# Small-head attention: lays ahead of waits, turned peaks in a scores bank, output projection ahead of the next scores

## The chip, the cores and the metric

The kernel runs on one core of one Trainium2 chip. The metric is the device time of one execution in microseconds, lower is better. The times of before are 7645.25, 7623.12 and 7643.76, median 7643.76.

## What is computed

A residual stack of eight blocks on x (32 samples of 128 tokens, 128 features), with a condition vector and a context of 77 tokens for each sample. The change touches attention with 16 heads of 8 features. It occurs once in the experts block (self attention, no mask) and twice in each of the six layers of the fourth conditioning block:

```python
for i in range(6):
    xn = _adaln(x, noise_emb, n1_w[i], n1_b[i])
    q, k, v = ...            # q and k turned by _rope
    a = _attn(q, k, v, src_mask).reshape(B, L, D) @ so_w[i].T
    x = x + a
    xn = _adaln(x, noise_emb, n2_w[i], n2_b[i])
    q = _rope((xn @ cq_w[i].T).reshape(B, L, H, HD))
    k = _rope((context @ ck_w[i].T).reshape(B, LC, H, HD))
    v = (context @ cv_w[i].T).reshape(B, LC, H, HD)
    a = _attn(q, k, v, ctx_mask).reshape(B, L, D) @ co_w[i].T
    x = x + a
    xn = _adaln(x, noise_emb, n3_w[i], n3_b[i])
    x = x + gelu(xn @ f1_w[i].T + f1_b[i]) @ f2_w[i].T + f2_b[i]
```

`_attn` is softmax(q k' / sqrt(8) + mask) v for every sample and head. All is float32.

## The kernel before, in words

Stages follow each other with a barrier between; each writes the queue of every engine by hand, and the engines meet only at semaphores. `stage_attn_experts` (E) holds the small attention of the experts block, `stage_layers` (H) the six layers in a hardware loop: self attention, cross attention, feed-forward.

One **unit** of the small attention is one sample, 32 units (B) in an attention. The 16 heads are four row groups of the TensorE array (32 rows, one PSUM bank each) by four masked key copies `km`. Per unit:

- `scores(u)` on PE: with a mask, four one-row matmuls that lay the mask into banks 0 to 3 (L178), then four matmuls that add the scores (L182).
- `peaks(u)` on DVE (L260): the row maxima, banks 0 and 1 first (this signals `half_peaked`), then 2 and 3. `split_peaks` (L267, L268) makes two bf16 parts of them and signals `peaks_ready`.
- `turn_peaks(u)` on PE (L190) transposes the peaks into columns 0 to 127 of bank PEAKS, which is 7. `spread_peaks(u)` on DVE (L273) makes `shift` from it and signals `shift_ready`.
- `again(u)` on PE computes the scores once more, transposed, keys on partitions, into banks 0, 1, 4 and 5: first four lays of the shift (L202), then 16 matmuls (L206).
- `exponential(u, half)` on ACT (L302), two halves, banks 0 and 1, then 4 and 5, each signals `exp_done`.
- `values(u, half)` on PE (L220) into bank FLAT, which is 6; `flatten` on ACT (L310) copies it out; `flip(u)` on PE (L228) transposes it back; `norm(u)` on DVE (L279, L280) divides by the sums.

Banks 0 and 1 are shared by the scores and by `again`; banks 2 and 3 belong to the scores alone, 4 and 5 to `again` alone.

The order of iteration u on PE is `turn_peaks(u)`, `scores(u+1)`, `values(u-1)` twice, the caller's `meanwhile(u)`, `again(u)`, `flip(u-1)`. On DVE it is `peaks(u)`, `split_peaks(u)`, `meanwhile(u)`, `norm(u-2)`, `spread_peaks(u)`. On ACT: `flatten(u-1)`, `meanwhile(u, 0)`, both exponentials, `meanwhile(u, 1)`.

In the layers `meanwhile` carries the output projection of pairs of units. On PE, `outputs(a, p, 0)` at even u from 4 transposes two samples into columns 256 to 511 of bank 7 (L2592), after waiting for `o_normed` and for `mix_added` of pair p-1; `outputs(a, p, 1)` at odd u from 5 multiplies them by the output weights in the same columns (L2598), after waiting for `oT_ready`. ACT copies between the two (`take_out`, L2729). On DVE, `add_outputs(a, (u-6)//2)` at even u from 6 adds the product to `y_all` (L2824), signals `mix_added` and takes row statistics (L2448); at every fourth u it takes their moments (L2454, L2456). As turned peaks and projection share bank 7, `area_free` makes `turn_peaks` wait until the other engine has left it. In stage E, `meanwhile` is on DVE only: the residual addition of four samples (L1763).

At the start of each attention twelve matmuls of no use (`keep_clock`, L161) follow `scores(0)`.

## Time and profile before

| | |
|---|---|
| times, us | 7645.25, 7623.12, 7643.76 |
| profiled execution: span, first to last instruction | 7609.3 us |
| profiled execution: own device time | not recorded apart from its span |
| PE matmul busy | 6115.0 us (80%) |
| DVE busy | 4921.5 us (65%) |
| ACT busy | 2873.3 us (38%) |
| mean granted TensorE clock | 0.838 |
| L182 of stage E, first to last start | 2311.3 to 2468.6 |
| L182 of the six layers, first to last start | 4422.0 to 7386.6 |

The span is one profiled execution; the times are whole executions, with what lies before the first and after the last instruction. An engine's busy share is a mean over stages with different limits, so the attention stretches are read by themselves: the distance from one L178 of PE to the next is the period of a unit.

### The profile page before, as it was taken

To read this page: it belongs to the slowest core of one execution; us is meant where nothing else is said; L and a number is where in the kernel's file an instruction comes from. 1 tells how busy PE (TensorE), PEld (TensorE's weight loads), DVE (VectorE), ACT (ScalarE), POOL (GpSimd) and SP (SyncE) were. 2 spreads that over 40 slices of the span, in tenths; PEclk is the share of its full clock that TensorE was granted. 3 is DMA by queue.
4 is the path that set the end of the run, shared out by engine and by line. 5 is a ranking of instruction groups with operands and counts; after the bars stand their busy time and mean duration, and the time that the engine had idled before them with its cause. 6 is when DMAs were issued, how large, how long until landed. Compare 5 with 4: busy or idle time off the path is not lost. (4 is left out here: it accounts for less than half of the span.)

```text
span 7609.3 us, 209213 instructions
## 1 busy us (share of the span) xinstructions
PE 6115.0 (80%) x89189; PEld 4582.1 (60%) x89189; DVE 4921.5 (65%) x17941; ACT 2873.3 (38%) x4943; POOL 1031.6 (14%) x932
## 2 busy tenths in 40 slices
PE   4454569889878798898989788888888888888887
PEld 3343446666665688888857555556556566555655
DVE  6777964554567766666644477577576675775864
ACT  1221224444425211111112155455456455554563
POOL 1113521221200200000000011101110111111101
PEclk7666779999989655555589899999999989999998
DMA  1000000000000000000000000000000000000000
GB/s 33 1 0 3 1 29 1 1 1 1 1 5 2 6 4 4 4 4 4 4 23 1 14 7 2 10 3 2 11 2 2 11 2 7 6 2 11 2 2 15
DMA packets 61311, 45.99 MB, mean 6 GB/s; under 512 B 22521, under 2 KB 56125, under 8 KB 60227
## 3 DMA queue, kind: packets, MB, share of 16 engines
q1 hardware_dynamic: 60355, 32.26, 1.6%
q8 instruction: 720, 11.80, 0.6%
q14 instruction: 236, 1.93, 0.1%
HBM read 30.14 MB, written 2.10 MB: 4 GB/s over the span
## 5 line engine op out<-in xcount | busy, mean ns | idle before, releaser
L260 DVE TENSOR_REDUCE peak<-ps 128x8 f32<-128x1024 f32 (+1 forms) x832 | 816.5, 1023 | 260.4 <-PE ps L182 259.8
L302 ACT ACTIVATE e<-ps,H_lowT_c 77x1024 f32<-77x1024 f32 x384 | 405.2, 1104 | 257.7 <-PE ps L206 257.7
L302 ACT ACTIVATE e<-ps,H_lowT_s 128x1024 f32<-128x1024 f32 x384 | 406.7, 1110 | 247.8 <-PE ps L206 247.8
L220 PEld LDWEIGHTS ps<-e,H_vt 128*32 128x32 f32 (+1 forms) x12288 | 318.7, 111 | 254.3 <-ACT e L302 138.3
L220 PE MATMUL ps<-e,H_vt 128*32 128x128 f32 (+1 forms) x12288 | 431.1, 281 | 23.6 <-DVE xs L280 17.7
L2460 POOL TENSOR_TENSOR H_rstd<-H_veps,neghalf 128x4 f32<-128x4 f32 (+1 forms) x146 | 160.8, 1101 | 2114.0 <-DVE H_veps L2456 2114.0
L206 PE MATMUL ps<-H_qr,H_km 32*128 32x128 f32 (+1 forms) x12288 | 421.9, 275 | 0.0
L206 PEld LDWEIGHTS ps<-H_qr,H_km 32*128 32x128 f32 (+1 forms) x12288 | 407.9, 170 | 15.0 <-issue 1.7
L2154 ACT ACTIVATE F_ex<-ps,F_nm 16x77 f32<-16x77 f32 x256 | 81.2, 317 | 825.3 <-DVE F_nm L2060 825.3
L1992 PE MATMUL ps<-F_hp,F_encW 128*128 128x1 bf16 (+2 forms) x12288 | 363.9, 166 | 34.4 <-issue 32.2
L310 ACT ACTIVATE oT<-ps 128x512 f32<-128x512 f32 x416 | 248.4, 597 | 347.2 <-PE ps L220 347.2
L2022 PE MATMUL ps<-F_eT,F_ctxp 77*128 77x1 f16 (+1 forms) x12288 | 375.2, 165 | 2.3
L2022 PEld LDWEIGHTS ps<-F_eT,F_ctxp 77*128 77x128 bf16 x12288 | 354.2, 104 | 25.6
L1992 PEld LDWEIGHTS ps<-F_hp,F_encW 128*128 128x128 bf16 x12288 | 347.7, 104 | 35.6 <-issue 35.6
L182 PE MATMUL ps<-H_km,H_qr 32*128 32x512 f32 (+1 forms) x3072 | 346.3, 518 | 0.0
L279 DVE RECIPROCAL den<-ps 128x16 f32<-128x16 f32 x416 | 107.0, 257 | 302.1 <-PE ps L228 299.2
L273 DVE TENSOR_TENSOR shift<-ps,own_row 128x512 bf16<-128x512 f32 x416 | 282.9, 680 | 17.2 <-PE ps L190 17.2
L228 PE MATMUL ps<-ident,oT 128*128 128x128 f32 x1664 | 277.3, 290 | 4.9 <-ACT oT L310 4.9
L2278 PEld LDWEIGHTS ps<-G_w,G_hid 128*128 128x128 f32 x2048 | 238.7, 192 | 20.2 <-issue 18.6
L2000 PE MATMUL ps<-F_hp,F_ph 128*128 128x16 bf16 x4608 | 241.7, 175 | 0.0
L2278 PE MATMUL ps<-G_w,G_hid 128*128 128x128 f32 x2048 | 239.0, 275 | 0.0
L2251 PE MATMUL ps<-G_nT,G_w 128*128 128x512 f32 x512 | 232.1, 597 | 0.0
(637 smaller groups left out, 13964.4 us busy)
## 6 DMA issues: line engine op xcount, KB each, us to landing
G_w<-in_L_ffn_w SPq DMA_DIRECT2D x16, 256.0 KB
H_f<-in_L_xcond_f_w SPq DMA_DIRECT2D x12, 256.0 KB
H_nw<-in_L_xcond_n_w SPq DMA_DIRECT2D x21, 128.0 KB, 2.1
A_cond<-in_cond SPq DMA_DIRECT2D x1, 2048.0 KB
out_x<-x_all SPq DMA_DIRECT2D x1, 2048.0 KB, 8.7
ctx_rows<-in_ctx SPq DMA_DIRECT2D x1, 1232.0 KB
D_wq<-in_L_xcond_attn_wq SPq DMA_DIRECT2D x2, 512.0 KB
D_wk<-in_L_xcond_attn_wk SPq DMA_DIRECT2D x2, 512.0 KB
```

The source lines that it names most:

```text
L182: last = nc.tensor.matmul(view(r), q_of(u)[rows(r), :], km_of(u)[rows(r), :, :], start=(low_of is None), stop=True, skip_group_check=True)
L206: last = nc.tensor.matmul(ps[0:keys, bank(r), s * S:(s + 1) * S], km_of(u)[rows(r), s, :], q_of(u)[rows(r), :], start=False, stop=True, sk ...
L220: last = nc.tensor.matmul(ps[PAD_COLS * s:PAD_COLS * (s + 1), FLAT, r * S:(r + 1) * S], vt_of(u)[0:keys, QUAD * r + s, :], e[0:keys, half, ...
L228: last = nc.tensor.transpose(ps[:, FLAT, r * S:(r + 1) * S], oT[:, r * S:(r + 1) * S], ident[:, :])
L260: last = nc.vector.tensor_reduce(peak[:, HL * half:HL * (half + 1)], view, AX.X, ALU.max, negate=True)
L273: nc.vector.tensor_tensor(shift[:], ps[:, PEAKS, 0:S].unsqueeze(1).broadcast_to([128, QUAD, S]), own_row[:].unsqueeze(2).broadcast_to([128 ...
L302: nc.scalar.activation(e[0:keys, half, :], ps[0:keys, AGAIN[half]:AGAIN[half] + 2, :].rearrange("p b t -> p (b t)"), ACT.Exp, bias=low(u) ...
L310: nc.scalar.activation(oT[:], ps[:, FLAT, :], ACT.Copy).then_inc(sem["o_read"], 1)
L1992: last = nc.tensor.matmul(scored(k)[:, 3 * j:3 * j + 3 - i], encW[:, i, b, :], hp[:, b, 0:3 - i], start=(i == 2 and j == 0), stop=(i == 0) ...
L2000: nc.tensor.matmul(gate(k, i if i < 2 else 3), gate_p["h"][:, a, i * D:(i + 1) * D], hp[:, mine(c), b], start=(i == 0 and a + b == 0), sto ...
L2022: last = nc.tensor.matmul(attended_bank(k)[:, 2 * j:2 * j + m], ctxp[:, i, CB * c + j, :], eT[:, c, j, 0:m], start=(i == 2 and j == 0), st ...
L2278: last = nc.tensor.matmul(per(OUT + m % 2)[:, u, :], hid[:, m % 2, c, u * S:(u + 1) * S], w2[:, x, c, :], start=False, stop=(c == 3), skip ...
```

## The change

In `scores`, the lays of banks 2 and 3 are issued before the wait for `exp_done`, those of banks 0 and 1 behind it; a wait for `shift_ready` N is added at its head. In `again`, the lays of banks 4 and 5 are issued before the wait for `half_peaked`, those of banks 0 and 1 behind it. PEAKS moves from bank 7 to bank 3; the projection keeps bank 7, under the name OUTS, and `area_free` goes. On PE `meanwhile(u)` moves from between `values` and `again` to between `turn_peaks(u)` and `scores(u+1)`, and loses its wait for `shift_ready`. On DVE `meanwhile(u)` moves behind `spread_peaks(u)`; the one of stage E comes one unit earlier.

```diff
--- before.py
+++ after.py
@@ -152,7 +152,7 @@
         HP = HD + 1
 
         PAD_COLS = 32
-        AGAIN, SPARE, FLAT, PEAKS = (0, 4), 2, 6, 7
+        AGAIN, SPARE, FLAT, PEAKS, OUTS = (0, 4), 2, 6, 3, 7
         AREA = slice(256, 512)
 
         def keep_clock(n, bank):
@@ -161,7 +161,7 @@
                 nc.tensor.matmul(ps[:, bank, 0:2 * S].rearrange("p (s k) -> p s k", s=2), ones_b[:],
                                  ones_b[:].unsqueeze(1).broadcast_to([128, 2, S]), start=True, stop=True, skip_group_check=True)
 
-        def small_tensor(pe, first, units, keys, q_of, km_of, vt_of, low_of, ready, ready_values, meanwhile=None, area_free=None):
+        def small_tensor(pe, first, units, keys, q_of, km_of, vt_of, low_of, ready, ready_values, meanwhile=None):
 
             rows = lambda r: slice(ROWS * r, ROWS * (r + 1))
 
@@ -170,14 +170,21 @@
                 ready(u)
                 if N >= 1:
                     pe.wait_ge(sem["peaks_ready"], N)
-                if N >= 2:
-                    pe.wait_ge(sem["exp_done"], 2 * N - 3)
+                    pe.wait_ge(sem["shift_ready"], N)
                 view = lambda r: ps[:, r, :].rearrange("p (s k) -> p s k", s=QUAD)[:, :, 0:keys]
-                if low_of:
-                    for r in range(QUAD):
+
+                def lay(r):
+                    if low_of:
                         nc.tensor.matmul(view(r), ones_b[ROWS * r:ROWS * r + 1, :],
                                          low_of(u)[ROWS * r:ROWS * r + 1, :].unsqueeze(1).broadcast_to([1, QUAD, keys]),
                                          start=True, stop=False, skip_group_check=True)
+
+                lay(2)
+                lay(3)
+                if N >= 2:
+                    pe.wait_ge(sem["exp_done"], 2 * N - 3)
+                lay(0)
+                lay(1)
                 for r in range(QUAD):
                     last = nc.tensor.matmul(view(r), q_of(u)[rows(r), :], km_of(u)[rows(r), :, :],
                                             start=(low_of is None), stop=True, skip_group_check=True)
@@ -185,22 +192,26 @@
 
             def turn_peaks(u):
                 pe.wait_ge(sem["peaks_ready"], first + u + 1)
-                if area_free:
-                    area_free(u)
                 nc.tensor.matmul(ps[:, PEAKS, 0:S], peak_parts[:], ident_b[:], start=True, stop=True).then_inc(sem["peaks_turned"], 1)
 
             def again(u):
 
                 N = first + u
                 pe.wait_ge(sem["shift_ready"], N + 1)
-                if u + 1 < units:
-                    pe.wait_ge(sem["half_peaked"], N + 2)
                 if N >= 1:
                     pe.wait_ge(sem["exp_done"], 2 * N)
                 bank = lambda r: AGAIN[r // 2] + r % 2
-                for r in range(QUAD):
+
+                def lay(r):
                     nc.tensor.matmul(ps[0:keys, bank(r), :].rearrange("p (s t) -> p s t", s=QUAD), ones_b[ROWS * r:ROWS * r + 2 * QUAD, 0:keys],
                                      shift[ROWS * r:ROWS * r + 2 * QUAD, :, :], start=True, stop=False, skip_group_check=True)
+
+                lay(2)
+                lay(3)
+                if u + 1 < units:
+                    pe.wait_ge(sem["half_peaked"], N + 2)
+                lay(0)
+                lay(1)
                 for s in range(QUAD):
                     for r in range(QUAD):
                         last = nc.tensor.matmul(ps[0:keys, bank(r), s * S:(s + 1) * S], km_of(u)[rows(r), s, :],
@@ -232,14 +243,13 @@
             keep_clock(12, FLAT)
             for u in range(units):
                 turn_peaks(u)
+                if meanwhile:
+                    meanwhile(u)
                 if u + 1 < units:
                     scores(u + 1)
                 if u:
                     values(u - 1, 0)
                     values(u - 1, 1)
-                if meanwhile:
-                    pe.wait_ge(sem["shift_ready"], first + u + 1)
-                    meanwhile(u)
                 again(u)
                 if u:
                     flip(u - 1)
@@ -283,11 +293,11 @@
             for u in range(units):
                 peaks(u)
                 split_peaks(u)
-                if meanwhile:
-                    meanwhile(u)
                 if u >= 2:
                     norm(u - 2)
                 spread_peaks(u)
+                if meanwhile:
+                    meanwhile(u)
             norm(units - 2)
             if meanwhile:
                 meanwhile(units)
@@ -1756,7 +1766,7 @@
                                 nc.vector.tensor_scalar(km[:, 0, m, :], kr[:, mine(0)], heads[:, m:m + 1], None, ALU.mult).then_inc(sem["masked_v"], 1)
 
                         def during(u):
-                            if u % U == 2 and u > U:
+                            if u % U == 1 and u > U:
                                 g = u // U - 1
                                 dve.wait_ge(sem["o_normed"], U * g + U)
                                 xg = x_all[:, g * U:(g + 1) * U, :]
@@ -2589,13 +2599,13 @@
                                     if PAIRS * a + p:
                                         pe.wait_ge(sem["mix_added"], PAIRS * a + p)
                                     for k in range(2):
-                                        last = nc.tensor.transpose(ps[:, PEAKS, AREA.start + k * S:AREA.start + (k + 1) * S],
+                                        last = nc.tensor.transpose(ps[:, OUTS, AREA.start + k * S:AREA.start + (k + 1) * S],
                                                                    o8[:, (2 * p + k) % U, :], ident[:])
                                     last.then_inc(sem["o_turned"], 1)
                                 else:
                                     pe.wait_ge(sem["oT_ready"], PAIRS * a + p + 1)
                                     for k in range(2):
-                                        last = nc.tensor.matmul(ps[:, PEAKS, AREA.start + k * D:AREA.start + (k + 1) * D],
+                                        last = nc.tensor.matmul(ps[:, OUTS, AREA.start + k * D:AREA.start + (k + 1) * D],
                                                                 o8T[:, p % 2, k * S:(k + 1) * S], w[m][:], start=True, stop=True)
                                     last.then_inc(sem["mix_done"], 1)
 
@@ -2609,15 +2619,6 @@
                                     elif u >= 5:
                                         outputs(a, (u - 5) // 2, 1, m)
                                 return pieces
-
-                            def area_free(a):
-
-                                def waits(u):
-                                    if u % 2 == 0 and u >= 6:
-                                        pe.wait_ge(sem["mix_added"], PAIRS * a + (u - 6) // 2 + 1)
-                                    elif u % 2 and u >= 5:
-                                        pe.wait_ge(sem["oT_ready"], PAIRS * a + (u - 5) // 2 + 1)
-                                return waits
 
                             def attend(a, keys, low, m):
                                 def ready(u):
@@ -2638,7 +2639,7 @@
                                 small_tensor(pe, B * a, B, keys, lambda u: qr[:, u * S:(u + 1) * S],
                                              lambda u: km[:, (u // U) % 2, :, (u % U) * keys:(u % U + 1) * keys],
                                              lambda u: vt[:, (u // U) % 2, u % U], lambda u: low[:, u * keys:(u + 1) * keys],
-                                             ready, ready_values, during(a, m), area_free(a))
+                                             ready, ready_values, during(a, m))
 
                             for n in range(3):
                                 for c in range(2):
@@ -2726,7 +2727,7 @@
                             def take_out(a, p):
 
                                 act.wait_ge(sem["o_turned"], PAIRS * a + p + 1)
-                                nc.scalar.activation(o8T[:, p % 2, :], ps[:, PEAKS, AREA], ACT.Copy).then_inc(sem["oT_ready"], 1)
+                                nc.scalar.activation(o8T[:, p % 2, :], ps[:, OUTS, AREA], ACT.Copy).then_inc(sem["oT_ready"], 1)
 
                             def take_rows(r, g):
 
@@ -2821,7 +2822,7 @@
 
                                 dve.wait_ge(sem["mix_done"], PAIRS * a + p + 1)
                                 at = slice(2 * p, 2 * p + 2)
-                                nc.vector.tensor_tensor(y_all[:, at], y_all[:, at], ps[:, PEAKS, AREA].rearrange("p (u d) -> p u d", u=2),
+                                nc.vector.tensor_tensor(y_all[:, at], y_all[:, at], ps[:, OUTS, AREA].rearrange("p (u d) -> p u d", u=2),
                                                         ALU.add).then_inc(sem["mix_added"], 1)
                                 dve.wait_ge(sem["mix_added"], PAIRS * a + p + 1)
                                 step(row_statistics(lambda u: y_all[:, u, :], range(at.start, at.stop)))
```

## Rows read from the trace of the kernel before

**Rows 1.** The page: its first line.

```profile
span 7609.3 us, 209213 instructions
```

**Rows 2.** The chain of waits in the six layers: who waited for whom, total us, times, longest.

```profile
PE ps L178 <- ACT e L302: 245.6, 360, 1.1
```

**Rows 3.** Timeline, self attention, two units: start us, us, engine, line, op, operands, [idle before].

```profile
4503.41 0.40 PE L178 MATMUL ps<-H_low_s,ones_b 1*128 1x512 bf16 x4 [0.67 <-ACT e L302]
...
4503.62 1.04 PE L182 MATMUL ps<-H_km,H_qr 32*128 32x512 f32 x8
...
4506.05 0.40 PE L202 MATMUL ps<-shift,ones_b 8*128 8x512 bf16 x4
...
4507.77 0.22 PE L190 MATMUL ps<-ident_b,peak_parts 128*128 128x128 bf16 x1
...
4508.47 0.68 DVE L273 TENSOR_TENSOR shift<-ps,own_row 128x512 bf16<-128x512 f32 x1
...
4508.67 0.40 PE L178 MATMUL ps<-H_low_s,ones_b 1*128 1x512 bf16 x4 [0.68 <-ACT e L302]
...
4510.86 0.71 PE L2598 MATMUL ps<-H_so_w,H_o8T 128*128 128x128 f32 x4
...
4511.51 0.40 PE L202 MATMUL ps<-shift,ones_b 8*128 8x512 bf16 x4
...
4512.68 0.41 DVE L2824 TENSOR_TENSOR H_y<-H_y,ps 128x256 f32<-128x256 f32 x1
```

**Rows 4.** Timeline, cross attention, two units with the output projection.

```profile
4722.82 0.31 PE L178 MATMUL ps<-H_low_c,ones_b 1*128 1x308 bf16 x4 [0.69 <-ACT e L302]
...
4725.24 0.41 PE L202 MATMUL ps<-shift,ones_b 8*77 8x512 bf16 x4
...
4727.86 0.32 PE L178 MATMUL ps<-H_low_c,ones_b 1*128 1x308 bf16 x4 [0.69 <-ACT e L302]
...
4729.64 0.44 PE L2592 MATMUL ps<-ident,xs 128*128 128x128 f32 x2
...
4730.01 0.41 PE L202 MATMUL ps<-shift,ones_b 8*77 8x512 bf16 x4
```

**Rows 5.** Timeline, cross attention, an early unit without the projection.

```profile
4664.38 0.32 PE L178 MATMUL ps<-H_low_c,ones_b 1*128 1x308 bf16 x4 [0.68 <-ACT e L302]
...
4666.40 0.41 PE L202 MATMUL ps<-shift,ones_b 8*77 8x512 bf16 x4 [0.17 <-issue]
```

**Rows 6.** Timeline, small attention of the experts stage.

```profile
2400.39 0.40 PE L202 MATMUL ps<-shift,ones_b 8*128 8x512 bf16 x4 [0.37 <-issue]
...
2402.80 0.68 DVE L273 TENSOR_TENSOR shift<-ps,own_row 128x512 bf16<-128x512 f32 x1
...
2402.91 1.14 PE L182 MATMUL ps<-E_km,E_qr 32*128 32x512 f32 x8 [0.59 <-ACT e L302]
```

**Rows 7.** Windows, attention stretches of three layers: stretch, length, busy by engine, PEclk, DMA.

```profile
4418.00:4440.00 22.00, 16.48 (x184) 9.76 (x182) 13.21 (x21) 6.84 (x9) 3.51 (x4) 0.84 0.14 34
...
4660.00:4813.00 153.00, 128.75 (x2671) 92.55 (x2667) 106.41 (x296) 98.73 (x135) 10.47 (x13) 1.00 0.01 3
6188.00:6236.00 48.00, 41.63 (x509) 28.57 (x513) 23.34 (x55) 17.94 (x24) 2.10 (x3) 0.57 0.01 2
```

**Rows 8.** Timeline, cross attention of the fourth layer, clock at its lower level.

```profile
6213.21 0.45 PE L178 MATMUL ps<-H_low_c,ones_b 1*128 1x308 bf16 x4 [0.18 <-ACT e L302]
...
6216.48 0.65 PE L202 MATMUL ps<-shift,ones_b 8*77 8x512 bf16 x4
...
6220.18 0.45 PE L178 MATMUL ps<-H_low_c,ones_b 1*128 1x308 bf16 x4 [0.18 <-ACT e L302]
...
6220.43 0.68 DVE L273 TENSOR_TENSOR shift<-ps,own_row 128x512 bf16<-128x512 f32 x1
```

**Rows 9.** Timeline, first units of the first self attention.

```profile
4425.92 0.23 PE L190 MATMUL ps<-ident_b,peak_parts 128*128 128x128 bf16 x1 [1.48 <-DVE peak_parts L268]
...
4428.79 0.40 PE L202 MATMUL ps<-shift,ones_b 8*128 8x512 bf16 x4 [1.45 <-DVE peak L260]
```

## The prediction

> **What bounds the kernel now.** The page gives a span of 7609.3 us [rows 1]. All edits lie in the small attention, which runs 13 times: once in stage E, 12 times in the layers, 32 units each. So I read the timeline of single units. The waits of the layers name the party that releases a unit's head [rows 2]: PE's mask lay (L178) waits for ACT's exponential, 245.6 us in 360 of 384 units.
>
> The timeline shows it as a ring [rows 3]. Call S the start of a unit's scores (L178) and T the start of `again` (L202). From S 4503.41 to T 4506.05 are 2.64 us: scores, first half of the maxima, `half_peaked`. From T to the next S, 4508.67, are 2.62: `again`, first exponential, `exp_done`. A unit takes 5.26. At odd u the projection's matmuls (L2598, 4510.86 plus 0.71) push T to 4511.51, 2.84 after S, and the unit takes 5.46.
>
> The row that matters most is the one that today matters nothing. `spread_peaks` (L273) starts at 4508.47 and takes 0.68, so it ends at 4509.15: 3.10 after T, and 0.48 **after** the next scores have started. It is late because `norm(u-2)` stands ahead of it in DVE's queue, and `norm` waits for `flip`, which PE issues behind `again`. Nobody but `again`, 2 us later, waits for it.
>
> **The change part by part.**
>
> *Wait for `shift_ready` in front of the scores.* With the turned peaks in bank 3, `scores(u+1)` may not touch that bank before `spread_peaks(u)` has read it. The wait stands at the head of `scores`, so lays and scores of all four banks queue behind it, and behind them on PE `values` and `again`. The next S becomes T + 3.10 + one handover from DVE to PE. I take 0.11 for the handover (bounds 0.05 and 0.2: after a maximum of half of 2.36 us DVE hands `half_peaked` over in about that). So T to S is 3.21 in place of 2.62: **+0.59** for each unit that has `norm` ahead, that is u = 2 to 30, 29 of them. The exponential, which ends before, is no bound any more.
>
> *Projection in front of the scores, on DVE behind `spread_peaks`.* Nothing here issues a DMA, and POOL gets its row moments (L2460) about a microsecond later in a queue that is mostly idle. The old place costs 0.20 at odd u in self attention (T 2.84 after S, against 2.64) [rows 3]. In cross attention the maxima are shorter and both places cost: T is 2.42 and 2.15 after S [rows 4], against 2.02 where no projection is in the way [rows 5]. That comes back: 0.20 for 13 units of a self attention (2.6 us), 0.40 + 0.13 for 13 pairs of a cross attention (6.9 us). In the new place the odd part (L2598, 0.71) fits between the end of the turned peaks (L190, 4507.77 + 0.22, so T + 1.94) and `shift_ready` (T + 3.21), where PE would idle 1.27: nothing. The even part does not. `outputs(a, p, 0)` at iteration u waits for `mix_added` of pair p-1, which DVE adds in its `meanwhile` of the **same** u; this now stands behind `spread_peaks(u)`. So at even u from 6, 13 units, PE waits for `spread_peaks`, then for the addition (L2824, 0.41 [rows 3]), then does the two transposes, which take 0.37 until the next operation can start (4729.64 to 4730.01 [rows 4]), and only then the scores. Less 0.1 by which DVE overlaps neighbours: **+0.68** a unit. Bounds: 0.37 if the addition were free, 0.9 if `spread_peaks` and addition do not overlap and the handover is a second 0.11. Behind the addition DVE still has its row statistics, but its next maxima wait for scores that end over 1 us after S.
>
> *Lays ahead of the waits.* The four lays take 0.40 together, as long as one, and the scores start 0.21 after the first lay [rows 3]: the row groups run side by side, each its lay, then its scores. After the change groups 0 and 1 still hold lay and scores behind the wait, and the maxima wait for the last matmul. I take 0, for both places. Bounds: a loss of 0.05, a gain of 0.21 in `scores`; L182's start, which group 0 sets, is the row nearest to what will run.
> The Trainium skill (TensorE: Matmul & The Clock Gate, Step-by-step) says that only weight loads are pulled ahead and matmuls stay in program order. By it the gain is 0; if row groups ran apart it would be up to 0.21 a unit for two groups of four, and still 0 for the slowest.
>
> *`area_free` gone.* The turned peaks come after `flip` on PE, and not later than `mix_added` or `oT_ready`; nothing.
>
> *Stage E.* No mask, no projection on PE. T 2400.39, `spread_peaks` ends at 2402.80 + 0.68 = 2403.48, next S (L182) 2402.91 [rows 6]: T + 3.20 in place of T + 2.52, **+0.68**, 29 times: +19.7 us. Moving the residual addition saves nothing, as it hid behind the exponential.
>
> **The sum.** Self attention: 29 × 0.59 − 2.6 + 13 × 0.68 = 23.3, six times: 140. Cross attention, same wait and T to S 2.62 as well: 17.1 − 6.9 + 8.8 = 19.0, six times: 114. Stage E 20. Together 274: the span goes from 7609.3 to 7883. The execution's own time is not recorded apart; the median of before is 34.5 above the span and I add the difference to it: 7643.8 + 274 = **7918** before the clock is counted.
>
> **The clock.** Cross attention runs mostly at full clock (1.00 over 153 us), but in the fourth layer 48 us have a mean of 0.57 [rows 7], mostly at the 1.2 GHz level. There T is 3.27 after S and the next S 3.70 after T [rows 8]: 6.97 a unit in place of 5.04 and 2.15 + 2.62 = 4.77. With the new wait: `spread_peaks` starts at 6220.43, ends 4.63 after T, so 3.27 + 4.74 = 8.0, against 2.02 + 3.21 = 5.23 at 2.4 GHz. The change leaves PE idle for about 1.3 us in a unit without projection and, from T + 1.94 to the end of the addition, for 1.6 at even u. The clock fell early in the first self attention (0.84 over that window [rows 7]) around two PE waits of 1.48 and 1.45 us [rows 9]. So it can fall more often, and come back later, as PE is busier before a rise today than it will be. The likeliest is that one cross attention in six, as today, is caught at the low level, but for its whole length: 27 units × 2.8 = 75 us, less what it costs today: 48 us hold seven units of 6.97, and seven times 2.1 are 14, of which I take 8, as the first units of a stage wait for other things: +67. Forecast 7918 + 67, about **7985**.
> The Trainium skill (TensorE: Matmul & The Clock Gate, A second HAM failure mode) describes a kernel whose short idles between groups of matmuls made the clock swing; its section What's actually happening lets it fall only after an idle window. By the second the time is 7918, by the first it is the third rival.
>
> **The rivals.**
>
> 1. *Schedule only, clock untouched:* 7918, and down to about 7810 if PE's even part finds `mix_added` in time (without 12 × 13 × 0.68 = 106). For: both waits are single microseconds. Chance 0.30.
> 2. *Faster.* The wait for `shift_ready` is hidden: if `spread_peaks` ended by T + 2.5, the ring would stay with the exponential, and the changes give back 2.6 and 6.9 a layer (57 us) and, with lays at 0.21 for 12 × 31 units, 78 more: about 7509. It decides at the point where `flip` and `norm` end 0.6 earlier than now. Against: the order `again`, `flip`, `norm`, `spread_peaks` is unchanged, and the row shows 3.10. Chance 0.03.
> 3. *The clock is lost in most cross attentions.* Three to six of them at 8.0 and more a unit: 7918 + 3 × 75 = 8140 to 7918 + 6 × 75 = 8370. For: the waits above; against: full clock over 153 us with waits of 0.7 us. Chance 0.22.
> 4. *Nothing comes of it,* as the added wait is nearly always passed: 7644. Only if L273's record were late by 0.5 us. Chance 0.02.
>
> The forecast, one or two cross attentions at the low level (7950 to 8090), has 0.43.
>
> **The numbers.** About 0.3% (23 us) is what a measurement of this kernel can tell from no change. The range 7870 to 8280 holds the forecast, most of rival 1 and more than half of rival 3; the low end is the schedule alone with the even part at its lower bound, 13 × 12 × 0.31 = 48 less. Faster 0.03, within 0.3% 0.02, slower 0.95.
>
> **What would show it.** In the changed profile PE's head of a unit (the first lay of `scores`) is released by DVE's L273, not by ACT; L178 follows `again` by 3.2 us at odd u and by 3.9 at even u; the transposes of the projection are released by DVE's addition; the chain of waits has `exp_done` no longer in front of the scores; PEclk in cross attention below 1.0 for whole stretches in one or two layers. The forecast is wrong if the first lay still follows the exponential, if even and odd units are equally long (then the addition is no wait), or if PEclk stays as it is.

## The result and the profile after

The changed kernel takes 8021.4 us (median of four, 8013.2 to 8025.1), the kernel before beside it 7644.5 (median of four): ratio **1.0505** (95% interval 1.0482 to 1.0527), +377 us. The forecast was 7985. The two traced executions stand 410 us apart: the span of before [rows 1], 7609.3, lies below all four of its times (7623.1 to 7654.6), while the span after is within 3 us of its median. So shares taken from the traces add up to 410, and prices in medians to 377. The ratio stands for 386.

The page after: span, engines, granted clock in forty slices, and the maxima.

```profile
span 8018.9 us, 208680 instructions
...
PE 6339.7 (79%) x89189; PEld 4731.9 (59%) x89189; DVE 4926.6 (61%) x17941; ACT 2873.8 (36%) x4943; POOL 1031.5 (13%) x932
...
PEclk7667788999898555555898988989889999988989
...
L270 DVE TENSOR_REDUCE peak<-ps 128x8 f32<-128x1024 f32 (+1 forms) x832 | 817.0, 1024 | 521.4 <-PE ps L189 521.2
```

DVE's and ACT's work is as before. PE is busy 225 us more (it was 6115.0), and the maxima now stand behind 521 us of waiting for the scores, where they had 260. PEclk has eights along the whole right half.

I call a unit's length the time from one S to the next. In this section and in the experiments it is read from the first score matmul of one unit (L182 before, L189 after) to that of the next, as some kernels issue lays ahead of their waits; in the steady units of before and after the two readings agree to 0.02. Of two lengths with a slash the first is an odd u, the second an even one, both with the projection (u from 6) and at full clock. Between the first and the last S of each attention, over the whole kernel:

| us | before | after | difference |
|---|---|---|---|
| experts stage | 157.2 | 180.3 | +23 |
| six self attentions | 998.3 | 1220.3 | +222 |
| six cross attentions | 943.4 | 1098.9 | +155 |
| of these at the low clock, self | 20.5 | 256 | +235 |
| the same, cross | 109 | 268 | +159 |

The first three rows are 400 of the 410 us.

The chain of waits in the layers after (who waited for whom, total us, times, longest):

```profile
PE ps L2602 <- DVE H_y L2825: 255.3, 156, 1.6
...
PE ps L178 <- DVE shift L283: 188.9, 216, 1.3
```

It replaces [rows 2]: PE's first lay (L178) follows DVE's `spread_peaks` (L283), and at even u the transposes (L2602) follow the residual addition (L2825), 156 times, which are 13 in each of the 12 attentions. The exponential (L312) no longer releases L178 anywhere in the list.

Timeline after, a self attention, an odd and an even unit (the same kind of view as [rows 3]):

```profile
4566.32 0.40 PE L178 MATMUL ps<-H_low_s,ones_b 1*128 1x512 bf16 x4 [0.81 <-DVE shift L283]
...
4567.51 1.08 PE L231 MATMUL ps<-e,H_vt 128*32 128x128 f32 x32
...
4568.53 0.81 PE L206 MATMUL ps<-shift,ones_b 8*128 8x512 bf16 x4
...
4568.94 0.09 PEld L206 LDWEIGHTS ps<-shift,ones_b 8*128 8x128 bf16 x2 [0.33 <-DVE peak L270]
...
4571.35 0.68 DVE L283 TENSOR_TENSOR shift<-ps,own_row 128x512 bf16<-128x512 f32 x1
4571.95 0.41 DVE L2825 TENSOR_TENSOR H_y<-H_y,ps 128x256 f32<-128x256 f32 x1
...
4572.51 0.41 PE L2602 MATMUL ps<-ident,xs 128*128 128x128 f32 x2 [1.64 <-DVE H_y L2825]
...
4572.85 0.40 PE L178 MATMUL ps<-H_low_s,ones_b 1*128 1x512 bf16 x4
...
4574.03 1.74 PE L231 MATMUL ps<-e,H_vt 128*32 128x128 f32 x32
...
4575.71 0.61 PE L206 MATMUL ps<-shift,ones_b 8*128 8x512 bf16 x4
...
4579.89 0.40 PE L178 MATMUL ps<-H_low_s,ones_b 1*128 1x512 bf16 x4 [0.81 <-DVE shift L283]
```

From S 4566.32 to T and on to `shift` at 4572.03 (4571.35 + 0.68) is the ring. The first two lays of `again` no longer wait for `half_peaked` and start at 4568.53; the other two do, and load at 4568.94, 2.62 after S, where T was 2.64 after S before. Then come the addition (to 4572.36), the transposes 0.15 later, and S at 4572.85, so this unit takes 6.53. **Look at L231:** the same 32 matmuls that take 1.08 at full clock (at 4567.51) take 1.74 behind the wait of 1.64. From 4574.30 to 4577.70 the granted clock is 0.50, the 1.2 GHz level, and the next S comes 7.04 later instead of 5.9.

Timeline after, a cross attention, for [rows 4]:

```profile
4778.36 0.32 PE L178 MATMUL ps<-H_low_c,ones_b 1*128 1x308 bf16 x4 [0.81 <-DVE shift L283]
...
4780.15 0.41 PE L206 MATMUL ps<-shift,ones_b 8*77 8x512 bf16 x4
...
4782.56 0.68 DVE L283 TENSOR_TENSOR shift<-ps,own_row 128x512 bf16<-128x512 f32 x1
4783.16 0.41 DVE L2825 TENSOR_TENSOR H_y<-H_y,ps 128x256 f32<-128x256 f32 x1
...
4783.72 0.41 PE L2602 MATMUL ps<-ident,xs 128*128 128x128 f32 x2 [1.64 <-DVE H_y L2825]
...
4784.06 0.31 PE L178 MATMUL ps<-H_low_c,ones_b 1*128 1x308 bf16 x4
```

T is 1.79 after S; `shift` is ready at 4783.24, 3.09 after T. S follows at 4784.06, which is 0.82 after `shift`. At 4778.36 above, without the addition in between, the same handover (from 4777.54 + 0.68 = 4778.22) took 0.14.

Windows of the first self and cross attention of the layers: stretch, length, busy us (with counts) of PE, PEld, DVE, ACT, POOL, then granted clock, DMA share, GB/s. Before:

```profile
4422.00:4591.00 169.00, 144.07 (x2653) 98.42 (x2649) 131.66 (x278) 101.50 (x130) 9.78 (x13) 0.98 0.03 7
4641.00:4798.00 157.00, 131.75 (x2656) 94.14 (x2659) 108.67 (x286) 96.55 (x130) 9.80 (x13) 0.96 0.01 3
```

After:

```profile
4449.00:4653.00 204.00, 163.16 (x2631) 108.73 (x2631) 131.37 (x277) 101.52 (x131) 10.22 (x13) 0.90 0.02 5
4703.00:4890.00 187.00, 146.25 (x2631) 106.17 (x2631) 108.65 (x287) 96.76 (x131) 10.28 (x13) 0.86 0.01 2
```

### The profile page after: what moved, and what is told of

Read it like the earlier page. It is cut to its first block and busy times, and to the rows that moved or that the text cites. A ratio compares the mean times of both kernels' runs of the same rounds, so it can differ in the third digit from the quotient of the medians.

```text
span 8018.9 us, 208680 instructions
## 1 busy us (share of the span) xinstructions
PE 6339.7 (79%) x89189; PEld 4731.9 (59%) x89189; DVE 4926.6 (61%) x17941; ACT 2873.8 (36%) x4943; POOL 1031.5 (13%) x932
## 5 line engine op out<-in xcount | busy, mean ns | idle before, releaser
L231 PEld LDWEIGHTS ps<-e,H_vt 128*32 128x32 f32 (+1 forms) x12288 | 363.8, 123 | 272.6 <-issue 238.8
L217 PE MATMUL ps<-H_qr,H_km 32*128 32x128 f32 (+1 forms) x12288 | 511.8, 304 | 0.0
L231 PE MATMUL ps<-e,H_vt 128*32 128x128 f32 (+1 forms) x12288 | 497.4, 310 | 16.4 <-DVE xs L290 11.3
L312 ACT ACTIVATE e<-ps,H_lowT_s 128x1024 f32<-128x1024 f32 x384 | 406.7, 1110 | 246.0 <-PE ps L217 246.0
L217 PEld LDWEIGHTS ps<-H_qr,H_km 32*128 32x128 f32 (+1 forms) x12288 | 477.5, 193 | 18.2 <-issue 6.2
L312 ACT ACTIVATE e<-ps,H_lowT_c 77x1024 f32<-77x1024 f32 x384 | 405.1, 1104 | 217.6 <-PE ps L217 217.6
L189 PE MATMUL ps<-H_km,H_qr 32*128 32x512 f32 (+1 forms) x3072 | 369.7, 550 | 0.0
L239 PE MATMUL ps<-ident,oT 128*128 128x128 f32 x1664 | 294.1, 303 | 4.9 <-ACT oT L320 4.9
L283 DVE TENSOR_TENSOR shift<-ps,own_row 128x512 bf16<-128x512 f32 x416 | 283.4, 681 | 20.9 <-PE ps L195 20.9
L2602 PE MATMUL ps<-ident,xs 128*128 128x128 f32 x384 | 80.1, 291 | 255.3 <-DVE H_y L2825 255.3
L206 PE MATMUL ps<-shift,ones_b 8*128 8x512 bf16 (+1 forms) x1664 | 259.9, 458 | 16.6 <-DVE peak L270 10.7
```

Of the source, the lines that this page charges most:

```text
L189: last = nc.tensor.matmul(view(r), q_of(u)[rows(r), :], km_of(u)[rows(r), :, :], start=(low_of is None), stop=True, skip_group_check=True)
L206: nc.tensor.matmul(ps[0:keys, bank(r), :].rearrange("p (s t) -> p s t", s=QUAD), ones_b[ROWS * r:ROWS * r + 2 * QUAD, 0:keys], shift[ROWS ...
L217: last = nc.tensor.matmul(ps[0:keys, bank(r), s * S:(s + 1) * S], km_of(u)[rows(r), s, :], q_of(u)[rows(r), :], start=False, stop=True, sk ...
L231: last = nc.tensor.matmul(ps[PAD_COLS * s:PAD_COLS * (s + 1), FLAT, r * S:(r + 1) * S], vt_of(u)[0:keys, QUAD * r + s, :], e[0:keys, half, ...
L239: last = nc.tensor.transpose(ps[:, FLAT, r * S:(r + 1) * S], oT[:, r * S:(r + 1) * S], ident[:, :])
L283: nc.vector.tensor_tensor(shift[:], ps[:, PEAKS, 0:S].unsqueeze(1).broadcast_to([128, QUAD, S]), own_row[:].unsqueeze(2).broadcast_to([128 ...
```

## The experiments

Filler matmuls are matmuls of no use that keep PE busy; they write to a bank that nobody reads then. Ratios are to the kernel before, run beside each. "e2" and so on are the labels' first parts.

**e1: the lays alone.** The new `lay(r)` order in `scores` and `again` (the first and the third part of the diff), without the wait for `shift_ready`, the bank and the moves.

> The kernel before with only the lays taken ahead of the waits, in scores and in again. The prediction said 0 for both places (7644). The trace of the changed kernel already speaks for a gain in cross attention: there again starts 1.78 us after the scores, against 2.02 without a projection in the way before. Theory A (a gain where the wait of again is met late, in cross attention only): 0.1 to 0.2 for 31 x 6 units, 20 to 40 us, 7605 to 7625. Theory B (row groups run apart, every unit gains 0.2): 7644 - 0.2 x 31 x 13 = 7563. Theory C (the split costs, as the maxima start 1.35 after S in place of 1.32): up to 12 us slower.

Measured: 7576.9 us, ratio 0.9931 (0.9909 to 0.9954). It is faster, so the forecast's 0 for the lays is wrong. Self units went from 5.26/5.47 to 5.15/5.37, cross units from 4.77/5.04 to 4.67/4.95, and cross units without projection from 4.57 to 4.31.

Timeline of before, the second unit of [rows 3], two more lines:

```profile
4507.41 2.12 ACT L302 ACTIVATE e<-ps,H_lowT_s 128x1024 f32<-128x1024 f32 x2 [0.79 <-PE ps L206]
...
4509.99 2.35 DVE L260 TENSOR_REDUCE peak<-ps 128x8 f32<-128x1024 f32 x2 [0.84 <-PE ps L182]
```

Timeline of e1, one unit in self attention:

```profile
4518.31 2.12 ACT L314 ACTIVATE e<-ps,H_lowT_s 128x1024 f32<-128x1024 f32 x2 [0.78 <-PE ps L218]
...
4518.80 0.39 PE L177 MATMUL ps<-H_low_s,ones_b 1*128 1x512 bf16 x2
...
4519.48 0.39 PE L177 MATMUL ps<-H_low_s,ones_b 1*128 1x512 bf16 x2 [0.29 <-ACT e L314]
...
4519.50 1.23 PE L188 MATMUL ps<-H_km,H_qr 32*128 32x512 f32 x8
...
4520.81 2.36 DVE L272 TENSOR_REDUCE peak<-ps 128x8 f32<-128x1024 f32 x2 [0.78 <-PE ps L188]
```

Half of the exponential ends at 4518.31 + 1.06 = 4519.37. The second pair of lays starts 0.11 later, and the first scores 0.02 after it, in place of 0.20 and 0.21 [rows 3]. Yet the maxima start 1.44 after that half exponential, against 1.52 before (4507.41 + 1.06 to 4509.99): of the 0.28 only 0.08 reaches DVE, as it waits for the last matmul (4519.50 + 1.23 = 4520.73).

**e9: only the lays of `scores`.**

> The kernel before with the lays ahead of the wait in scores alone, not in again. It splits the gain of 0.69% of both. Theory (what is saved is the time from the exponential's end to the first operation behind it, 0.19 before and 0.11 with both lays, as the change of tile shape is done ahead): self units 5.26 to 5.18, nothing in stage E, which has no mask: 7628 - 0.08 x 31 x 12 = 7600. Rival (again's lays bring it all): 7628.

Measured: 7600.2, ratio 0.9961 (0.9948 to 0.9975). Self 5.18/5.37, cross 4.67/4.95, stage E as before (5.05, it has no mask). Two of its cross attentions have 44 us of low clock and take 163.5, where the others take 152 to 153; these 22 us are nearly all that it is behind e1 and e12. So by the unit lengths most of the gain is in `scores`. `again` gives 0.03 at odd u of self attention, 0.04 in stage E, and more in the few units without projection (cross 4.49 in e9, 4.31 in e1). There the row of before has [0.17 <-issue] in front of the lays although `values` is through [rows 5]; in e1 the same lays start before `values` ends, and T is 1.77 after the second pair of mask lays, where it was 2.02 after S.

**e12: is it the lays' own time, or what stands ahead of them?** All four lays stay behind the wait, and one further mask matmul is put ahead of it.

```diff
                     pe.wait_ge(sem["peaks_ready"], N)
+                if low_of:
+                    nc.tensor.matmul(ps[:, 3, :].rearrange("p (s k) -> p s k", s=QUAD)[:, :, 0:keys], ones_b[ROWS * 3:ROWS * 3 + 1, :],
+                                     low_of(u)[ROWS * 3:ROWS * 3 + 1, :].unsqueeze(1).broadcast_to([1, QUAD, keys]),
+                                     start=True, stop=True, skip_group_check=True)
                 if N >= 2:
                     pe.wait_ge(sem["exp_done"], 2 * N - 3)
```

> The kernel before with one more mask matmul into bank 3 ahead of the wait for exp_done in scores; all four lays stay behind it. Theory (what lays ahead save in scores is the change to 32-row shapes after a full-array matmul, 0.08 a unit): the same gain as lays ahead in scores alone, about 0.4%, 7600. Rival (the gain comes from there being two lays less behind the wait): no gain, 7628.

Measured: 7578.0, ratio 0.9926 (0.9912 to 0.9940), as good as e1, with one matmul more. Self 5.18/5.37, cross 4.67/4.95, exactly as in e9.

Timeline of e12, the same place:

```profile
4519.64 2.12 ACT L306 ACTIVATE e<-ps,H_lowT_s 128x1024 f32<-128x1024 f32 x2 [0.81 <-PE ps L210]
...
4520.15 0.38 PE L174 MATMUL ps<-H_low_s,ones_b 1*128 1x512 bf16 x1
...
4520.81 0.40 PE L182 MATMUL ps<-H_low_s,ones_b 1*128 1x512 bf16 x4 [0.28 <-ACT e L306]
...
4521.03 1.03 PE L186 MATMUL ps<-H_km,H_qr 32*128 32x512 f32 x8
```

Half of the exponential ends at 4520.70. The four lays start 0.11 later and the maxima (4522.14) 1.44 later, exactly as in e1, though all lays are behind the wait. So what is hidden is not the lays' 0.40 us but 0.08 that goes with the **first** small matmul after the turned peaks. The turned peaks use the whole array (128x128) and the lays one row of 32. The Trainium skill (TensorEngine Tiling (Array Packing), Key Properties) says that a change of tiling mode drains TensorE; the rows agree with a price of 0.08 us here. That it is the drain, and not another cost of the first instruction in a shape, no run tells apart.

**e2: the bank alone.** Kernel before, with PEAKS in bank 3 and the wait that it forces; `area_free` goes, as in the change.

```diff
-        AGAIN, SPARE, FLAT, PEAKS = (0, 4), 2, 6, 7
+        AGAIN, SPARE, FLAT, PEAKS, OUTS = (0, 4), 2, 6, 3, 7
@@ scores
                     pe.wait_ge(sem["peaks_ready"], N)
+                    pe.wait_ge(sem["shift_ready"], N)
```

> The kernel before with only the turned peaks moved to bank 3 and the wait for shift_ready ahead of the scores; projection and DVE order as before. Theory (the wait is the larger part): T to S becomes 3.21, and 3.44 at even u where the addition still stands ahead of norm. Self attention 5.86 and 6.05 + 0.23, cross 5.36 and 5.7; +122 + 109 + 20 = +250, 7895 with the clock at full, up to 7960 where it falls. Rival (the moved projection is the cause of the loss): under 7700.

Measured: 7982.3, ratio 1.0474 (1.0441 to 1.0506): +355 us in medians. This one wait, in the order of before, loses nearly as much as the whole change. That is above the 7960 of the expectation; the low clock holds 72 us of the self and 317 us of the cross attentions.

Timeline of e2, two units in self attention:

```profile
4530.89 0.68 DVE L272 TENSOR_TENSOR shift<-ps,own_row 128x512 bf16<-128x512 f32 x1
...
4531.82 0.40 PE L179 MATMUL ps<-H_low_s,ones_b 1*128 1x512 bf16 x4 [1.42 <-DVE shift L272]
...
4537.31 0.68 DVE L272 TENSOR_TENSOR shift<-ps,own_row 128x512 bf16<-128x512 f32 x1
...
4538.09 0.40 PE L179 MATMUL ps<-H_low_s,ones_b 1*128 1x512 bf16 x4 [1.49 <-DVE shift L272]
```

S (L179) is now 0.10 to 0.25 after the end of `shift` (L272), with PE idle for 1.4 to 1.5 us ahead of it.

**e3: DVE's `meanwhile` back ahead of `norm` and `spread_peaks`** (and stage E's addition at its old u), all else as changed.

```diff
                 split_peaks(u)
+                if meanwhile:
+                    meanwhile(u)
                 if u >= 2:
                     norm(u - 2)
                 spread_peaks(u)
-                if meanwhile:
-                    meanwhile(u)
```

> The changed kernel with DVE's meanwhile back ahead of norm and spread_peaks. Theory (PE's even transposes wait for the addition behind spread_peaks): even units go from 6.54 to about 6.1 in self and from 5.70 to about 5.13 in cross attention, 78 x 0.45 + 78 x 0.57 = 80 us, and the clock, which falls beside the long idle of even units, comes back for most of the time: 7850 to 7940. Rival (the addition was hidden): within 20 us of 8021.

Measured: 7875.4, ratio 1.0321 (1.0290 to 1.0352). The addition is no longer late: cross units 5.02/5.09 in place of 5.07/5.70, self 5.86/6.33 in place of 5.91/6.54. One wait stands for the whole ring now (waits of e3 in the layers):

```profile
PE ps L178 <- DVE shift L283: 381.0, 372, 1.3
```

All but 12 of the 384 heads of a unit follow `shift`. Between e2 and e3 stand the lays and PE's projection in its new place: 1.0474 to 1.0321, a **gain** of some 117 us (107 in medians). From e3 to the changed kernel the DVE order costs 1.84%, 141 us, with what it does to the clock.

**e5: `spread_peaks` ahead of `norm`,** all else as changed.

```diff
                 split_peaks(u)
+                spread_peaks(u)
                 if u >= 2:
                     norm(u - 2)
-                spread_peaks(u)
```

> The changed kernel with spread_peaks ahead of norm in DVE's queue, the addition still last. Theory (the wait costs because norm, which waits for flip, stands ahead of spread_peaks): spread_peaks then starts when the peaks are turned, 1.94 after T, and ends at 2.7, so odd units lose about 0.4: 5.45 in self and 4.65 in cross attention. The addition still follows norm, about 3.3 to 3.7 after T, so even units stay at 6.4 and 5.6. 0.4 x 16 x 13 = 80 us and part of the clock: 7860 to 7950. Rival (the wait for shift_ready has another cause, such as the handover): within 20 us of 8021.

Measured: 7924.3, ratio 1.0384 (1.0365 to 1.0403). Units at full clock without the addition drop from 5.86 and 5.91 to 5.42 and 5.48 in self attention, and from 5.02 and 5.07 to 4.59 and 4.63 in cross attention (each pair is without and with the projection). So `norm` ahead of `spread_peaks` is what made `shift` late, as the forecast had it. Even units do not: 6.59 and 5.76.

Timeline of e5, self attention, an even and an odd unit:

```profile
4550.74 0.69 DVE L283 TENSOR_TENSOR shift<-ps,own_row 128x512 bf16<-128x512 f32 x1 [0.47 <-PE ps L195]
4551.34 0.25 DVE L289 RECIPROCAL den<-ps 128x16 f32<-128x16 f32 x1
...
4552.39 0.41 PE L2602 MATMUL ps<-ident,xs 128*128 128x128 f32 x2 [1.69 <-DVE H_y L2825]
...
4559.33 0.40 PE L178 MATMUL ps<-H_low_s,ones_b 1*128 1x512 bf16 x4 [0.38 <-DVE shift L283]
```

`shift` is ready at 4551.43, but the transposes (L2602) start at 4552.39, as the addition now stands behind `norm`. In the odd unit the wait in front of L178 is 0.38.

**e4: the clock.** Filler matmuls in PE's idle time, all else as changed.

```diff
                 turn_peaks(u)
+                keep_clock(4, SPARE)
                 if meanwhile:
                     meanwhile(u)
```

> The changed kernel with four matmuls of no use after each turned peaks, in bank 2, which nobody reads then; 0.43 us in a wait of 1.27. They change no dependence. Theory (about 170 of the 377 us are the clock: self attention 202.7 against 189 by its full-clock units, cross 182 to 185 against 169): low stretches mostly vanish, odd units stay at 5.86 and 5.06, time 7860 to 7900. Rival (the loss is schedule alone, low stretches are a symptom that costs nothing): 8021 or more.

Measured: 7878.6, ratio 1.0330 (1.0299 to 1.0361). Four matmuls more per unit make the kernel 143 us **faster** in medians (134 by the ratios). The lengths at full clock are unchanged to 0.01 (self 5.91/6.54, cross 5.07/5.70), so the filler costs nothing and repairs nothing in the ring. Low clock: self 256 to 27 us, cross 268 to 133. (The traced execution of e4 is the fastest of its four, 7856.2 against a median of 7878.6, so its low clock may be below the usual.)

Windows of e4, same columns:

```profile
4428.00:4619.00 191.00, 161.52 (x2755) 109.00 (x2755) 131.36 (x277) 101.61 (x131) 10.29 (x13) 1.00 0.02 6
4668.00:4844.00 176.00, 148.56 (x2755) 109.30 (x2755) 108.85 (x287) 96.95 (x131) 10.28 (x13) 0.93 0.01 2
```

The first self attention is at 1.00 throughout.

So the clock is a price of its own. Which waits bring it down is less clear. Low clock behind the seventh S of each attention, in us (self + cross, one traced execution each): 0 + 14 in e4, 0 + 8 before, 191 + 104 in the changed kernel, 82 + 38 in e3, where no unit waits for the addition and the longest wait for `shift` is 1.3, 113 + 133 in e5, whose even units still wait up to 1.7, and 0 + 140 in e2, where PE waits 1.4 to 1.5 in the self attention units above. So the wait of 1.64 at even u is a large part of it and not the whole, and no single length of wait explains them all.

**e7, e8, e10: what the bank could be good for.** e1 for the experts stage and the self attentions. In cross attention (e7): turned peaks in bank 3, projection on PE ahead of the scores, and on DVE `meanwhile`, then `spread_peaks`, then `norm`.

> Lays ahead everywhere; experts stage and self attention otherwise as before the change; cross attention with the turned peaks in bank 3, the projection ahead of the scores, and DVE in the order addition, spread_peaks, norm. Theory (the new place of the projection is worth something where nothing waits for spread_peaks behind norm): T to S 2.8, S to T 1.78, units of 4.6 in cross attention against 4.81 with lays alone: about 7577 - 40 = 7540. Rival (the separate bank is worth nothing, as PE's own order limits): 7577 or slower, up to 7640 if the wait still costs 0.2 more a unit than the row of the turned peaks shows.

Measured: 7597.1, ratio 0.9952 (0.9937 to 0.9967). Cross units 4.59/4.66, better than e1's 4.67/4.95 and as expected, but the first ones lose it again (low clock 31 us in five of the six attentions, in e1 14): no gain over e1, where 7540 was expected.

e8 turns the peaks of the next unit ahead of `flip` in cross attention (against e7, added lines only; the old places are dropped):

```diff
                 again(u)
+                if apart and u + 1 < units:
+                    turn_peaks(u + 1)
                 if u:
                     flip(u - 1)
+                if apart and u + 1 < units:
+                    meanwhile(u + 1)
```

> As the previous kernel, with turn_peaks(u+1) ahead of flip(u-1) on PE in cross attention. Theory (spread_peaks can then end before the exponential, so the ring is again, exponential, scores and nothing else): T to S 2.6, units of 4.4 to 4.6 in cross attention, 7577 - 0.3 x 29 x 6 = about 7525, down to 7500. Rival (PE's queue is the bound, since flip and projection now stand behind the turned peaks): no better than the previous one.

Measured: 7545.4, ratio 0.9876 (0.9855 to 0.9897). Cross units 4.20/4.68. Timeline of e8, cross attention:

```profile
4745.47 0.32 PE L179 MATMUL ps<-H_low_c,ones_b 1*128 1x308 bf16 x4 [0.68 <-DVE shift L293]
...
4748.47 0.23 PE L198 MATMUL ps<-ident_b,peak_parts 128*128 128x128 bf16 x1
...
4748.54 0.61 PE L242 MATMUL ps<-ident,oT 128*128 128x128 f32 x4
...
4748.74 0.69 DVE L293 TENSOR_TENSOR shift<-ps,own_row 128x512 bf16<-128x512 f32 x1
...
4749.57 0.52 PE L179 MATMUL ps<-H_low_c,ones_b 1*128 1x308 bf16 x4
```

The turned peaks (L198) now stand ahead of `flip` (L242), and `shift` is ready at 4749.43. S follows 0.14 later at 4749.57, 4.10 after the last (4.20 between score matmuls), and at this odd u no wait is left in front of it, as the projection fills the time. At 4745.47, an even u, PE still waits 0.68 for `shift`.

e10 is e8 with the row statistics of the addition (L2448 of before) behind `spread_peaks` and `norm`.

> As the kernel with early turned peaks in cross attention, with the row statistics of the added output behind spread_peaks and norm in DVE's queue. Theory (its units of 4.68 are those in which addition and statistics, 0.9 us, stand ahead of spread_peaks; the others take 4.20): 4.68 becomes 4.25, 13 x 0.4 x 6 = 31 us less: about 7515. Rival (4.68 comes from PE's queue, where the projection now stands behind flip): 7545.

Measured: 7528.5, ratio 0.9860 (0.9842 to 0.9878); cross units 4.37/4.31. The interval overlaps that of e8, so of a gain over e8 I can only say that it is small. In the traces a cross attention goes from 149.6 to 146.1; the self attentions, whose code is the same, differ by up to 2.5 each through the clock (6.8 us low in five of them in e8, none in e10).

**e11: a warm start.** e10 with more filler at the head of each attention (`apart` is true in cross attention).

```diff
-            keep_clock(12, FLAT)
+            keep_clock(40 if apart else 12, FLAT)
@@ in the loop, behind scores(u + 1)
+                if u == 0:
+                    keep_clock(12, FLAT)
```

> As the previous kernel, with more matmuls of no use in the first unit of an attention: 40 in place of 12 behind the first scores of cross attention, 12 behind the second scores of each. They fill waits and change no dependence. Theory (the clock falls in the first units, after PE waits of 2 to 3 us, and the low stretch of 31 us costs 2.5 us in each of three to four units): 8 us a cross attention and 2.4 a self attention, 60 us less at most, 7455 to 7500. Rival (the clock falls for another reason, or the matmuls delay the first peaks): as the previous one or slower.

Measured: **7457.3, ratio 0.9763 (0.9747 to 0.9779)**, 71 us less than e10 and the fastest version here: 178 us less than the kernel before beside it. The first cross units take 6.47, 4.61, 4.31, where e10 had 6.46, 5.30, 6.87 and before 5.65, 6.26, 6.89. The self attentions take 161.5 from first to last S in both e10 and e11, without low clock in either, so there the added filler bought nothing.

Windows of e11:

```profile
4422.00:4585.00 163.00, 152.31 (x2641) 99.78 (x2641) 131.13 (x278) 101.65 (x131) 10.29 (x13) 1.00 0.03 7
4637.00:4775.00 138.00, 132.00 (x2675) 96.99 (x2679) 106.93 (x285) 96.42 (x130) 10.14 (x13) 1.00 0.01 3
```

Both attentions run at 1.00, and from first to last S the first cross attention takes 136.7 us (155.5 before, 185.5 after).

## Why the prediction was right, and where it was not

**The wait for `shift_ready`: right.** Forecast T to S 3.21 and a self unit of 2.64 + 3.21 = 5.85; measured 5.86 in the units ahead of the projection, and 5.91 at odd u behind it, where the scores follow directly on the transposes. The handover from DVE to PE was 0.14, forecast 0.11. e2 has the wait alone and 1.0474; e5 shows that `norm` in front of `spread_peaks` makes it bind. Stage E: forecast +20, measured +23.

**Even units waiting for the addition: right.** Forecast 5.85 + 0.68 = 6.53, measured 6.54; in cross attention 5.02 to 5.70, +0.68. e3 takes it away and with it 1.84%.

**Projection out of T's way: right in sign, larger in cross attention.** There 2.02 + 3.21 = 5.23 was forecast, and T came 1.79 after S, so 5.02 to 5.07. The 0.23 go with the lays of `again`: e1 has T about as early, and its units without projection are 0.18 shorter than those of e9.

**The lays: wrong.** The step that failed is "I take 0, for both places": it looked only at what the four lays take among themselves (0.40, side by side) and at the last row group. e1 gives −0.69%; e12 shows that in `scores` the gain comes with the first small matmul ahead of the wait, and e9's units that this is most of it. The premise that matmuls stay in program order does not hold for their starts here: in e1 the score matmul that comes last in the program is the sixth of eight to start. In the changed kernel `scores` gets none of the gain, as the lays stand behind `shift_ready`; and in self attention neither did `again` (5.84 in e2's shortest units, 5.86 after). So the failed step moved the sum by 0.23 a cross unit, an estimate of 40 us over 29 units of six attentions. In rival 2 the 0.21 a unit was too much: e1's units with projection lost 0.09 to 0.11.

**The schedule's sum: near.** Forecast 274. e4 has this schedule and spends 133 us at the low clock in its cross attentions, near the 109 of before; it stands 3.30% or 252 us above before. That it is so near owes something to luck: the lays took some 40 away that the sum did not have (as above), and some 18 came back from terms that no run separates. One self attention without low clock takes 189.9 in e4 and 165.3 before: +24.6, forecast +23.3.

**The clock: right in kind, wrong in place and size.** The step was "one cross attention in six, as today, is caught at the low level, but for its whole length", +67. No attention was caught for its whole length. Instead the clock fell and came back in all twelve, in the first units and then mostly right behind the wait at even u: 256 + 268 us at the low level, against 20 + 109. Today's clock was misread too: the row of 1.00 in [rows 7] starts at 4660, and the low stretch of that attention lies ahead of it. Five cross attentions of before have one of 13.7 us in their first units, the fourth 41. The forecast left the self attentions at full clock; they lost most, 222 where the schedule's terms give 140. The mis-sized term measured 134 to 143 (what e4's filler gives back), not 67. The two waits of 1.48 and 1.45 us in [rows 9], around which the clock had already fallen before, pointed at it: the change puts one of 1.64 into every second unit, and the forecast used them only to say that the clock could fall, and not to count how often. How often it would fall could not be read from them: e2 has such waits in self attention and keeps its clock there behind the seventh S.

The Trainium skill (TensorE: Matmul & The Clock Gate, A second HAM failure mode) describes what the timelines show, a clock that swings as PE idles shortly between groups of matmuls; the wait at even u here is 1.64 us. By its section What's actually happening, which wants an idle window, the time was to be 7918, and the runs speak against that.

**The rivals.** Rival 1 (7918) comes near e4 (7878.6, or 7896 by its ratio), which needs the filler for it. Rival 3 (most cross attentions lost) named the right direction and was not reached: every attention lost a part. Rival 2's turning point, `shift` 0.6 earlier, is what e8 makes in cross attention by turning the peaks ahead of `flip`; there `norm` no longer stands in front of `shift`, and the sign does turn (0.9876, against 0.9931 for the lays alone).

**The total.** Forecast +341 (274 + 67), measured +377 in medians and +386 by the ratio, of which e4 leaves 252 to the schedule and 134 to the clock. The schedule took some 22 less than forecast, the clock 67 more. The two errors partly cancelled, which is luck, and the result is 36 us above the forecast.

What stays open: which pattern of waits brings the clock down; turned peaks ahead of `flip` in self attention, which were not tried; and which of its two fillers helps cross attention in e11.

## What to carry to other kernels

Before a buffer is moved onto one that the critical engine writes next, look up when its reader ends, **even if nobody waits for that reader today**: 0.48 us of slack that was negative cost 4.7%. A wait in a loop has two prices, its own length and what the clock does with it; the second was over a third of the loss here, and the trace shows it as the same group of matmuls taking 1.74 instead of 1.08. If a wait can't be removed, filler in it (e4) or in the first units of a stage (e11) can pay. Moving the bank alone lost (e2); it paid here only once what stood in front of the late producer, `norm` and `flip`, stood behind it (e8).

## What the runs showed of the hardware

- One small matmul, of the shape that is to come, ahead of a wait is worth 0.08 us after it (e12), with the lays themselves left behind the wait.
- In e1 the first scores, of the row groups whose lays were done, started 0.02 after the last lays were issued and not 0.21: two row groups, while the other two started 0.22 after the lays (4519.70) and the maxima had to wait for them. In all 384 units of the layers in e1 and in the changed kernel, the score matmul that comes last in the program and signals is the sixth of eight to start; in before and in e12, where all lays stand together, it is the eighth. So, as the starts are recorded, matmuls of different row groups run apart, and a row group whose lay is done does not wait for its neighbours' lays.
- The granted clock fell in the middle of an attention with a wait of 1.64 us in every second unit, and four further matmuls in each unit kept it up in the six self attentions but for 27 us (256 without them), and in the cross attentions halved the low clock (268 to 133).
